# Decoder layer on one core: the attention operations of four batches in a new order on all engines, six copies on other engines, gate/up fills in other places

## The reference

```python
x = layernorm(x + self_attention(x))          # 16 heads, q/k/v of width 64, causal
x = layernorm(x + cross_attention(x, ctx))    # 16 heads of width 8, key mask, biases
x = layernorm(x + moe(x))                     # 8 experts, width 256, top-2 sparsemixer gates
# self_attention
scores = einsum('bhsq,bhtq->bhst', q, k); masked = where(causal, -inf, scores)
weights = softmax(masked / sqrt(64)); out = weights @ v; return cat(out) @ w_o.T
# moe, all experts dense
for e in range(8):
    h = silu(x @ w_gate[e].T) * (x @ w_up[e].T)
    out = out + dense_w[:, e:e+1] * (h @ w_down[e].T)
```

## Time and profile before

| | us |
|---|---|
| median of 3 runs | 356.63 |
| lowest, highest | 354.76, 358.93 |
| the profiled execution | 354.66 |
| its span | 352.8 |
| mean granted clock of PE in it | 0.920 of full |

### The profile page before, as it was taken

One profiled execution on the slowest core, in us unless ns is written; L12 is line 12 of the kernel. 1 busy time (PEld: TensorE's weight loads), 2 busy tenths in 40 slices (PEclk: granted clock), 3 DMA queues, 4 the chain that ended last, 5 costly groups with the idle time before them and its releaser, 6 DMA issues.

```text
span 352.8 us, 6733 instructions
## 1 busy us (share of the span) xinstructions
PE 271.9 (77%) x2222; PEld 225.0 (64%) x2222; DVE 184.1 (52%) x917; ACT 174.3 (49%) x570; POOL 98.8 (28%) x154
## 2 busy tenths in 40 slices
PE   0969777677867767868786788675968889899994
PEld 0957655454655545637475467454756789899994
DVE  3553345346445437534633663375247358757686
ACT  3365656665575465575446444644335836333200
POOL 2758351431342333062133212621020010001021
PEclk9989999999999989998988866988587899999998
DMA  7980000000000000000000000000000000000001
GB/s 268 305 352 1 4 0 0 2 1 3 0 2 1 2 2 1 1 2 0 2 2 2 0 0 2 1 1 2 0 2 1 0 2 3 1 2 15 2 16 30
DMA packets 6433, 9.07 MB, mean 26 GB/s; under 512 B 1024, under 2 KB 4736, under 8 KB 6016
## 3 DMA queue, kind: packets, MB, share of 16 engines
q1 hardware_dynamic: 4032, 7.09, 5.7%
q10 hardware_dynamic: 2368, 1.57, 1.5%
HBM read 8.14 MB, written 0.52 MB: 25 GB/s over the span
## 4 chain that ended last, share of the span: by engine, by line
PE 48%; ACT 22%; DVE 16%; issue 8%; POOL 3%; DMA 1%; POOLq 0%; DVEq 0%; ACTq 0%; SPq 0%
ACT probs_s L434 8%; PE bank L1276 6%; ACT probs_c L437 6%; PE bank L1126 6%; PE bank L1008 5%; PE bank L997 5%; PE bank L933 5%; PE bank L934 5%; PE bank L935 4%; DVE masked_c L627 3%; DVE masked_s L627 3%; PE bank L1061 3%; ACT xT_all L491 2%; PE bank L1085 2%; PE bank L1071 2%
## 5 line engine op out<-in xcount | busy, mean ns | idle before, releaser
L434 ACT ACTIVATE probs_s<-masked_s,nmax_s 128x128 f32<-128x128 f32 x128 | 49.9, 392 | 36.5 <-DVE nmax_s L627 27.6
L437 ACT ACTIVATE probs_c<-masked_c,nmax_c 128x128 f32<-128x128 f32 x128 | 40.8, 391 | 48.1 <-DVE nmax_c L627 38.9
L627 DVE CUSTOM_DVE_ANT_0 masked_s<-bank,causal 128x128 f32<-128x128 f32 x128 | 29.4, 286 | 38.8 <-PE bank L997 38.8
L299 POOL TENSOR_TENSOR probs_s<-probs_s,rec_sum_s 128x512 f32<-128x512 f32 x32 | 33.2, 1040 | 52.5 <-DVE rec_sum_s L634 52.5
L933 PE MATMUL bank<-ctx_hi,gu_hi 128*128 128x256 f32 x128 | 41.2, 322 | 1.0 <-DVE raw L720 1.0
L627 DVE CUSTOM_DVE_ANT_0 masked_c<-bank,mask_add 128x128 f32<-128x128 f32 x128 | 29.4, 286 | 19.0 <-PE bank L1008 18.9
L934 PE MATMUL bank<-ctx_lo,gu_hi 128*128 128x256 f32 x128 | 37.5, 293 | 0.0
L935 PE MATMUL bank<-ctx_hi,gu_lo 128*128 128x256 f32 x128 | 37.2, 291 | 0.0
L469 ACT ACTIVATE silu<-bank 128x256 f32<-128x256 f32 x51 | 19.3, 386 | 29.8 <-PE bank L935 29.7
L1061 PE MATMUL bank<-ident,probs_s 128*128 128x128 f32 x128 | 24.3, 320 | 12.0 <-POOL probs_s L299 8.6
L1061 PEld LDWEIGHTS bank<-ident,probs_s 128*128 128x128 f32 x128 | 15.9, 159 | 22.2 <-POOL probs_s L299 11.2
(11 more groups left out here) (152 smaller groups left out, 602.7 us busy)
## 6 DMA issues: line engine op xcount, KB each, us to landing
raw<-in_gateT SPq DMA_DIRECT2D x1, 1024.0 KB, 4.8
raw<-in_upT SPq DMA_DIRECT2D x1, 1024.0 KB, 7.0
down_sb<-in_down SPq DMA_DIRECT2D x1, 1024.0 KB, 9.0
raw<-in_wkT ACTq DMA_DIRECT2D x2, 256.0 KB, 4.6
raw<-in_wqT SPq DMA_DIRECT2D x2, 256.0 KB, 5.0
raw<-in_wvT SPq DMA_DIRECT2D x1, 512.0 KB, 6.1
ctxT_all<-in_ctxT SPq DMA_DIRECT2D x1, 512.0 KB, 7.3
wo_sb<-in_woT SPq DMA_DIRECT2D x1, 512.0 KB, 6.5
```

The lines of the kernel that those rows point to most:

```text
L299: pool.tensor_tensor(probs_s[:, g % 2], probs_s[:, g % 2], spread(rec_sum_s[:, 4 * g:4 * g + 4], 2, S), ALU.mult).then_inc(normed, 1)
L434: last = act.activation(probs_s[:, g % 2, i, :], masked_s[:, g % 2, i, :], ACT.Exp, scale=-1.0, bias=nmax_s[:, h:h + 1], accum_out=rsum_s[ ...
L437: last = act.activation(probs_c[:, g % 2, i, :], masked_c[:, g % 2, i, :], ACT.Exp, scale=-1.0, bias=nmax_c[:, h:h + 1])
L627: last = dve.tensor_tensor_reduce(out=masked[:, g % 2, i, :], in0=b[:, i * S:(i + 1) * S], in1=add, scale=-1.0, scalar=3e38, op0=ALU.add, ...
```

## The change

Everything computes what it did; the same instructions run but for the engine of six copies. It does this:

- **Order.** The loops run over `B + 2` (ACT, PE) or `B + 3` (DVE, POOL) iterations, every helper does nothing outside batches 0 to 7 (`on(n)`), and the tail behind the loop is gone. In iteration n the engines work on batches n+1, n, n-1, n-2 (DVE and POOL n-3 too).
- **Copies.** `evac_x1T`, `evac_oc`, `evac_x2T` and one of the four q/k copies of an iteration go from ACT to DVE; `evac_qc` and `evac_ccatT` go from DVE to ACT.
- **Slots.** `project_qk` has fixed banks X1, Y0, OC, Y1 and fixed places, `project_v` Y0 and X0; both `project_cv` and `project_kc` are done in iteration 0 ahead of `project_out_s`.
- **Fills.** 22 `gate_up`s instead of 26 stand ahead of the router's end, at places in iterations 7, 8 and 9 given by three tables; 10 instead of 6 follow behind `route(7)`. The first 10 take the tanh form.
- **POOL.** The pieces of `split_gu` are spread over iterations 1 to 6; `split_x2` and the roots move by one iteration.

```diff
+    GATE_PE = {(7, "turn_oc"): [0], (7, "turn_ccat"): [1], (7, "turn_x2"): [2], (7, "mix_c1"): [3], (7, "mix_c3"): [4, 5],
+               (8, "turn_oc"): [6], (8, "score_c1"): [7], (8, "turn_c0"): [8], (8, "turn_c1"): [9], (8, "route"): [10],
+               (8, "turn_c2"): [11, 12], (8, "mix_c3"): [13, 14], (9, "turn_oc"): [15, 16], (9, "turn_ccat"): [17, 18],
+               (9, "project_out_c"): [19, 20], (9, "turn_x2"): [21]}
+    GATE_DVE = {(7, "turned_s0"): [0], (7, "max_c0"): [1], (8, "res1"): [2], (8, "x1"): [3], (8, "oc"): [4], (8, "divide"): [5, 6],
+                (8, "max_c0"): [7], (9, "logits"): [8, 9, 10, 11, 12], (9, "oc"): [13, 14], (9, "divide"): [15, 16], (9, "res2"): [17, 18],
+                (10, "x2"): [19, 20], (10, "x2T"): [21]}
+    NFILL = 22
+    NTANH = 10
...
 # POOL
+            for n in range(B + 3):
+                for piece in GU_STEPS.get(n, ()):
+                    split_gu(piece)
+                if n > 0:
+                    own_k(n)
+                normalise(0, n)
+                root(var1_done, pow1_done, mv1, n - 1)
+                add_out_bias(n - 2)
+                normalise(1, n)
...
+                normalise(2, n)
+                normalise(3, n)
...
+                root(var2_done, pow2_done, mv2, n - 2)
+                padded_v(n - 1)
+                split_x2(n - 3)
...
 # ACT
+            for n in range(B + 2):
+                evac_turned_c(2, n - 2)
+                evac_turned_c(3, n - 2)
+                exp("s", 1, n)
+                evac_v(n, 1, X0 if n else T1)
+                evac_qk(n, 0)
+                exp("s", 2, n)
+                evac_qc(n - 1)
+                evac_ccatT(n - 2)
+                exp("s", 3, n)
+                evac_qk(n, 3)
+                evac_cat_first(n)
+                exp("c", 0, n - 1)
+                exp("c", 1, n - 1)
+                evac_qk(n, 2)
+                exp("s", 0, n + 1)
+                evac_turned_c(0, n - 1)
+                exp("c", 2, n - 1)
+                evac_turned_c(1, n - 1)
+                exp("c", 3, n - 1)
+                    evac_v(n + 1, 0, Y0)
...
 # DVE
+            for n in range(B + 3):
+                    group_max("s", 0, n)
+                normalise_x2(n - 3)
+                group_max("c", 2, n - 2)
+                evac_cat_last(n - 1)
+                evac_x2T(n - 3)
+                group_max("c", 3, n - 2)
+                evac_logits(n - 3)
+                group_max("s", 1, n)
+                reciprocal_s(0, n)
+                residual1(n - 1)
+                normalise_x1(n - 1)
+                evac_oc(n - 2)
+                group_max("s", 2, n)
+                reciprocal_s(1, n)
+                evac_x1T(n - 1)
+                group_max("s", 3, n)
+                divide_c(n - 2)
+                evac_turned_s(0, n)
+                evac_turned_s(1, n)
+                reciprocal_s(2, n)
+                residual2(n - 2)
+                reciprocal_s(3, n)
+                group_max("c", 0, n - 1)
+                group_max("c", 1, n - 1)
+                evac_qk1(n)
+                evac_turned_s(2, n)
+                evac_turned_s(3, n)
...
 # PE
+            for n in range(B + 2):
                 turn_s(0, n)
+                turn_oc(n - 2)
+                next_qk(n, 1, (maxed["s"], NG * n + 3))
+                project_qc(n - 1)
                 turn_s(1, n)
+                turn_ccat(n - 2)
+                next_qk(n, 3, (maxed["s"], NG * n + 4))
+                project_out_c(n - 2)
+                score_c(n - 1, 0)
+                mix_s(n, 0)
+                next_qk(n, 2, (res2_done, n - 1), (kc_evac, 1))
+                turn_s(2, n)
+                turn_s(3, n)
+                score_s(n + 1, 0)
+                score_c(n - 1, 1)
+                mix_s(n, 1)
+                turn_c(0, n - 1)
+                turn_c(1, n - 1)
+                turn_x2(n - 2)
+                project_v(n + 1, 0, Y0, (maxed["c"], NG * (n - 1) + 3), (qk_evac_v, min(n + 1, NSLOT)))
+                route(n - 2)
                 project_out_s(n)
+                mix_c(0, n - 1)
+                mix_c(1, n - 1)
+                turn_c(2, n - 1)
+                turn_c(3, n - 1)
+                project_v(n + 1, 1, X0, (maxed["s"], NG * (n + 1) + 1))
+                mix_c(2, n - 1)
+                mix_c(3, n - 1)
+                score_s(n + 1, 1)
+                next_qk(n + 1, 0, (maxed["s"], NG * (n + 1) + 2))
                 turn_x1(n)
```

More of the change, by code:

```diff
@@ new lines, in evac_qc @@
+            def evac_qc(n):
+                if on(n):
+                    act.wait_ge(cq_proj, n + 1)
+                    act.activation(qc[:], OS[:, 0:S], ACT.Identity, bias=cb_nat[:, 0:1]).then_inc(cq_evac, 1)
+            def evac_turned_c(j, m):
+                if on(m):
+                    act.wait_ge(turned["c"], NG * m + j + 1)
+                    if m == 0 and j == 0:
+                        act.wait_ge(x_split, 2 * NPAIR)
+                    wait(act, mixed["c"], NG * m + j - 1)
+                    act.copy(probsT_c[:, j % 2].rearrange("p h t -> p (h t)"), TURNED[j % 2][:]).then_inc(turned_evac["c"], 1)
@@ L591, in _ @@
+                exp("c", 3, n - 1)
+                gates(n, "exp_c3")
+                if n + 1 < B:
+                    evac_v(n + 1, 0, Y0)
+            for i in range(NFILL, 2 * KB):
                 gate(i)
@@ L946, in project_qk, with next_qk, project_v @@
                 last.then_inc(qk_proj, 1)
-            def project_v(n, c, b):
+            def next_qk(n, i, *free):
+                if 0 <= n < NSLOT:
+                    for s, v in free:
+                        wait(pe, s, v)
+                    project_qk(n // 2 + 1, 4 * (n % 2) + i, QK_BANK[i])
+            def project_v(n, c, b, *free):
+                if not on(n):
+                    return
+                for s, v in free:
+                    wait(pe, s, v)
                 if n == 0 and c == 0:
@@ L1087, in mix_s, with mix_c @@
                 last.then_inc(mixed["s"], 1)
-            def mix_c(j, m, b):
+            def mix_c(j, m):
+                if not on(m):
+                    return
                 pe.wait_ge(turned_evac["c"], NG * m + j + 1)
@@ L1229, in _ @@
-            turn_ccat(B - 2)
-            pe.wait_ge(hid_done, NIN + 2)
-            score_c(m, 1)
-            project_out_c(B - 2)
-            turn_c(0, m)
-            pe.wait_ge(maxed["c"], NG * m + 1)
-            gate_up(NIN + 2)
-            turn_c(1, m)
-            pe.wait_ge(maxed["c"], NG * m + 2)
-            gate_up(NIN + 3)
-            mix_c(0, m, OS)
-            mix_c(1, m, OS)
-            turn_x2(B - 2)
-            turn_c(2, m)
-            pe.wait_ge(maxed["c"], NG * m + 3)
@@ L1244, in _ @@
-            gate_up(NIN + 4)
-            turn_c(3, m)
-            pe.wait_ge(maxed["c"], NG * m + 4)
-            gate_up(NIN + 5)
-            route(B - 2)
-            mix_c(2, m, OS)
-            mix_c(3, m, OS)
-            gate_up(NIN + 6)
-            gate_up(NIN + 7)
-            pe.wait_ge(logit_evac, B - 1)
-            turn_oc(B - 1)
-            gate_up(NIN + 8)
-            gate_up(NIN + 9)
-            turn_ccat(B - 1)
-            gate_up(NIN + 10)
-            gate_up(NIN + 11)
@@ L1260, in _ @@
-            project_out_c(B - 1)
-            gate_up(NIN + 12)
-            gate_up(NIN + 13)
-            turn_x2(B - 1)
-            gate_up(NIN + 14)
-            gate_up(NIN + 15)
-            route(B - 1)
+                turn_ccat(n - 2)
+                gates(n, "turn_ccat")
+                next_qk(n, 3, (maxed["s"], NG * n + 4))
+                project_out_c(n - 2)
+                gates(n, "project_out_c")
+                score_c(n - 1, 0)
+                mix_s(n, 0)
+                if n == 0:
+                    pe.wait_ge(qk_evac_a, 1)
+                    project_cv(1, X1)
```

733 lines of the change are left out of this document (290 added, 443 removed).

## The result

| | before | after |
|---|---|---|
| median, us | 356.44 (354.76 to 358.93) | 267.88 (267.39 to 268.6) |
| ratio, 95% interval | | 0.7513 [0.7464, 0.7561] |
| span of the profiled execution, us | 352.8 | 265.8 |
| mean granted clock of PE | 0.920 | 0.973 |

The change takes a quarter of the time. Page of after: busy time and share of the engines, PE's busy tenths and PE's clock in 40 slices, and the shares of the chain that ended last.

What follows compares the result with a forecast made beforehand. The prediction took round-trip latency, not work, to bound the loop, with the expert stage PE-bound. Its terms, 179.9 + 33.5 + 64.4, gave 277.8 us of span, 279.7 with 1.9 outside it, and 281 as median; range 268 to 303.

Steps and rivals of the forecast that it cites:

- What bounds it: Old loop turns by latency, not work: PE idles 7.7 of 28.80 us in stretch 3, waiting on round trips between engines.
- The walk: One iteration, n from 2 to 5, followed through the four new orders: no slack negative, PE never idles, round 20.0 us.
- The length of a round: Stretches 2 to 5: 21.5 us a round, PE's column of 21.07 plus a little idle time; 86.0 us in all.
- The head: Up to `project_out_s(0)`: about 4 us of work moves in; bounds 33.7 and 38, taken as 36.5 us.
- Stretch 1: Second term: 17.7 us of PE work, taken as 18.9 us with fewer batches to cover each other; before 26.1.
- DVE's own waits: `normalise_x1` waits about 0.9 us for POOL's root, covered; POOL running beside the normalisations could add up to 11 us, taken as nothing.
- The copies: Six copies change engine: ACT 17.59 to 16.5 us a stretch, DVE 14.36 to 15.7; alone worth nothing, they matter as handovers.
- The late stretches: Stretches 6 and 7: forecast 19.0 and 19.5; rival keeps 36, 36 and 41 with the end: 322 us, chance 0.05.
- The end: Mark 7 to `route(7)`: 33.5 us including 1.7 for one clock fall; from `route(7)` to the end 64.4 us.
- The sum: Whole kernel: 179.9 + 33.5 + 64.4 = 277.8 us of span, against 352.8; median 281.
- Thin handovers: Rival: one late wait heading DVE's or ACT's order delays all behind it; rounds about 25 us, total 310, chance 0.22.
- The ring over two batches: Rival: dependencies tying four batches set the round by latency, 33.5 us, total 365; chance 0.05 with any other serialisation.

Runs made afterwards that it cites:

- the run with the late block: On PE, `score_s(n+1, 1)` and the q/k projection behind it moved past `turn_x1`, `turn_s(0)` and `turn_oc` in the changed kernel: 278.66 us.
- The kernel at 256.2 us of span: Changed kernel with POOL's pieces moved, `hidden(7)` later, `gate_up(9)` ahead of `turn_c(1)`, and `gate_up(7)`'s matmuls done three times: 258.52 us.

## Why the prediction was right or wrong, step by step

**What bounds it** was right. A round turned by latency: PE idled 7.7 of 28.8 us, and of 0.86 us more of PE's work half vanished in a wait. In the new order PE is the bound: it has no gap, and the same 0.86 is paid in full.

**The walk** was right in its verdict (PE finds all its inputs in a round, so even the thin slacks of 0.2 to 0.5 us held) but I didn't trust it. Only one block had to move for 1.2 us a round to come back.

**The length of a round** is the step that failed. I took 21.5 us, from the 21.07 of PE's busy column in stretch 3 of before, and called the sum of such columns, 250.6 + 13 = 264, the floor of any order. But the column is no measure of work. The same 195 to 198 instructions fill 21.07 us before, 20.05 in the run with the late block, 19.64 with two gaps a round, 19.30 with one, and 19.10 with none. The listed length of a matmul is longer than its distance to the next one that follows at once (0.28 against 0.12 us), and this surplus is laid open each time PE has to wait. From 10 gaps in stretch 3 of before and 1.97 us of surplus it is 0.20 us a gap. The column of the weight loads hardly moves, 15.68 us before and 15.62 after. The walk's start-to-start sum, 20.0, was nearer, though it too had blocks at too high a price: `project_out_c` at 0.42, which takes 0.31 in the round of after, and `project_qc`, 0.42 in stretch 3 of before and 0.22 in after. Stretches 2 to 5 came out 9.4 us below the forecast, of which 6.0 are the choice of 21.5 over 20.0 and 3.4 are 20.0 against 19.15; the same error is in stretches 6 (1.1) and 7 (1.3). The kernel at 256.2 us of span lies under the "floor" by 8 us. The Trainium skill warns of this (Perfetto Trace Analysis, "Identifying the Most-Contended Engine"): a matmul's busy time says little of how near TensorE is to its limit, because matmuls are pipelined, and it looks at the weight loads' instead. The rows agree, with their 1.97 us of surplus in one stretch and 0.06 in the weight loads. The reason that the Trainium skill gives there, that pipelined instructions look smaller in the trace, isn't what misled here: the column came out too large, 21.07 us for work that takes 19.10.

**The head**: 32.7 against my 36.5. I added 2.8 to the 33.7 of before as a middle between "hidden" and "not hidden"; the moved work of 4 us went wholly into PE's idle time (11.99 us busy of 12.70), as in the lower bound that I had named, 33.7. It came out 1.0 us below that bound; the 3.4 us of half clock that before has there (mean 0.88) are gone.

**Stretch 1**: 20.2 against 18.9. This is the one stretch where I had looked at no other order than PE's: the prediction doesn't walk POOL through iterations 0 and 1. The root at 39.02 shows the cost, and the run with POOL's pieces moved gives 16.1. So with that error removed this term too was over-estimated, by 2.8.

**DVE's own waits**: foreseen at 0.9 us behind `root`, measured 1.2, and costing nothing while PE's order covers it, as said. It ends later than I had it: not with the root, but with `add_out_bias` behind it, for `normalise_x1` writes the `x1` that this reads. That also keeps the two from running side by side, and the lengthening that I held possible doesn't come: `normalise_x1` takes 345 to 349 ns in all eight batches. `normalise_x2` is lengthened in two of eight, from 0.34 to 0.68 us (timelines of POOL and DVE):

```profile
107.27 0.62 POOL L336 CAST gu_hi<-raw 128x512 fp32r<-128x512 f32 x1
```

```profile
107.28 0.68 DVE L686 TENSOR_SCALAR ctxT_all<-res,mv 128x128 f32<-128x128 f32 x1
```

Both lengthened ones began 0.01 us behind a cast of POOL. This one ends at 107.96, 0.07 us behind the cast's end (107.89), and the `normalise_x1` of before ended 0.07 us behind its `own_k` as well (259.98 against 259.91). So such an operation ends with its partner, and isn't put behind it in full. Those rounds are as long as the others (19.2 us), so taking nothing for it was right.

**The copies** "alone are worth nothing": right in the old order (0.998), and wrong as a statement on the change, in which they are worth 6.8 us.

**The late stretches**: 17.9 and 18.2 us, against 36.3 and 36.5; the rival that gives them their old pace falls, and with it the idea that tanh fills make them slow. The clock there is 1.00.

**The end**: 35.9 against 33.5. The gap at `turn_c(1)` and its cause, `hidden(7)`, were foreseen at about 2 us; it came as 1.26. The 1.64 us at `turn_c(0)` were not foreseen. I charged one fall of the clock with 1.7 us; it stayed at half for 10.2 us, in which PE worked 8.55, so the fall cost some 4.3. `route(7)` to the end was 64.3 against 64.4.

**The sum**: -3.8 + 1.3 - 9.4 - 1.1 - 1.3 + 2.4 - 0.1 = -12.0 us of span. The rest of the 13.1 is the 0.6% by which the median before lay above its profiled execution; after, the two differ by 0.3 us.

**Rivals.** Thin handovers: rounds of 19.2 us, not 25. It is what DVE's load brings back if it rises by 2.7 us, at a smaller size. The ring over two batches: no sign of it; a block moved behind 0.9 us of work made a round 1.2 us longer, not more.

## What to carry to other kernels

Where every engine takes its queue in order and none is full, look for the round trips and put blocks of other batches behind each; ask first whether more work on the busiest engine is free. Read the answer block by block in a stretch of full clock (here one of two doubled transposes was free and the other paid), not from the total, which the clock can level out (0.997). Take a pipelined engine's work from start-to-start times in a stretch without gaps, never from its busy time in a stretch with gaps. Walk every queue in the first and last iterations as well, where one-time work (here 3.7 us of mask and the splits on POOL) stands in front of what the steady round needs.

## What the runs showed that I had not expected

**Not every gap brings the clock down.** Ahead of the fall at 179.9 us in after, and at the same place in the kernel with the doubled transposes, PE's activity is nearly the same. After (the stretch ahead and the fall), then the other (ahead and behind):

```profile
174.00:179.90 5.90, 3.59 (x25) 2.24 (x24) 3.90 (x18) 2.34 (x8) 2.07 (x5) 0.98 0.01 4
179.90:190.10 10.20, 8.55 (x50) 7.24 (x50) 5.22 (x33) 5.53 (x17) 0.00 (x0) 0.51 0.00 0
```

```profile
180.00:186.00 6.00, 3.64 (x26) 2.29 (x26) 4.01 (x18) 2.34 (x8) 2.07 (x5) 1.00 0.01 1
186.00:196.00 10.00, 7.75 (x79) 6.56 (x77) 5.38 (x34) 7.44 (x20) 0.00 (x0) 1.00 0.01 2
```

3.59 us of work in 5.90 was followed by 10.2 us at half clock, 3.64 in 6.00 by none. It is no chance of one execution: the mean clock is 0.973 in all four runs of after and 0.992 to 0.998 in those of the other. In the kernel with `hidden(7)` moved a wait of 1.63 us at that place was followed by 3.4 us of half clock in the profiled execution, while the mean clocks of its other three (0.996 to 0.998) leave no room for that. What decides stays open; after and the kernel with the doubled transposes differ in where in time the gap lies (6 us later) and in what PE does beside it. So the kernel with more PE work is 2.4 us faster than after in that part, and a change of 1 to 4 us in this kernel can be the clock's and not the edit's: look at the clock of both traces before reading such a difference.

**A queue head counts more than a queue's load.** DVE, with 15.4 of 19.1 us busy, had room for less than 2.7 us; ACT, with 16.7, took 0.95 and the rounds stayed at 19.2. The two additions were not of one size, so this is a comparison with the 3.7 and 2.4 us that the two seemed to have free, and no like-for-like test.
